# Issuing the two output stores of a pair from ScalarE instead of SyncE, in a two-layer graph attention kernel

## What is computed

```python
x = _layernorm(x + _L0_gnn_ref(x, adj, adj, Wq, Wk, Wv, bv, Wo, bo))   # scores + adj + adj, output projection
x = _layernorm(x + _L1_gnn_ref(x, adj, Wq, bq, Wk, bk, Wv, bv, beta))  # scores + beta*adj, masked where adj <= 0
# scores = q k^T * scale + bias;  probs = softmax(scores);  out = probs v
# layernorm(x) = (x - mean) / sqrt(var + 1e-5)
```

## Time and profile before

| | us |
|---|---|
| median of 3 runs | 2331.73 (2331.39 to 2332.79) |
| the profiled execution | 2332.92 |
| its span, first to last instruction | 2331.1 |
| PE busy | 2136.1 (92%) |
| DVE busy | 1876.7 (81%) |
| ACT busy | 1844.8 (79%) |
| POOL busy | 1558.9 (67%) |

### The profile page before, as it was taken

One profiled execution on the slowest core, in us unless ns is written; L12 is line 12 of the kernel. 1 busy time (PEld: TensorE's weight loads), 2 busy tenths in 40 slices (PEclk: granted clock), 3 DMA queues, 4 the chain that ended last, 5 costly groups with the idle time before them and its releaser, 6 DMA issues.

```text
span 2331.1 us, 86096 instructions
## 1 busy us (share of the span) xinstructions
PE 2136.1 (92%) x23808; PEld 1926.8 (83%) x23808; DVE 1876.7 (81%) x8451; ACT 1844.8 (79%) x7688; POOL 1558.9 (67%) x2188
## 2 busy tenths in 40 slices
PE   5899999999999999999999999999999999999973
PEld 5888888888888888888888888888888888888852
DVE  4688888888888888888888888888888888888763
ACT  5578888888888788788788788888888888887764
POOL 5666766776676776676676676676676676676652
PEclk9999999999999999999999999999999999999976
DMA  5255454454554554554554554544544544544443
GB/s 145 72 135 131 131 140 125 131 140 128 128 143 126 129 142 123 133 140 121 137 138 120 140 134 122 143 131 122 142 131 126 138 130 129 134 130 122 123 104 79
DMA packets 234654, 299.36 MB, mean 128 GB/s; under 512 B 26704, under 2 KB 226384, under 8 KB 234576
## 3 DMA queue, kind: packets, MB, share of 16 engines
q1 hardware_dynamic: 234576, 298.43, 49.4%
HBM read 46.67 MB, written 25.17 MB: 31 GB/s over the span
## 4 chain that ended last, share of the span: by engine, by line
PE 44%; issue 18%; ACT 15%; DVE 11%; POOL 8%; DMA 1%; ACTq 1%; DVEq 1%; POOLq 0%; SPq 0%
ACT prob L586 13%; PE r_bank L365 11%; PE r_bank L367 9%; PE r_bank L366 9%; PE s_bank L415 7%; DVE neg_s L697 5%; PE r_bank L431 4%; POOL flip L914 3%; PE r_bank L348 2%; DVE neg_max L697 2%; PE r_bank L358 1%; PE r_bank L443 1%; DVE y L763 1%; POOL rstd L863 1%; ACT o1T L558 1%
## 5 line engine op out<-in xcount | busy, mean ns | idle before, releaser
L586 ACT ACTIVATE prob<-neg_s,neg_max 128x128 f32<-128x128 f32 x3072 | 1192.1, 393 | 205.6 <-DVE neg_max L697 205.0
L697 DVE CUSTOM_DVE_ANT_0 neg_s<-s_bank,bias 128x128 f32<-128x128 f32 x3072 | 670.3, 286 | 145.8 <-PE s_bank L415 116.0
L586 ACT ACTIVATION_READ_ACCUMULATOR prob<-neg_s,neg_max 128x1 f32 x3072 | 589.9, 192 | 0.0
L932 POOL TENSOR_TENSOR prob<-prob,inv_sum 128x512 f32<-128x512 f32 x384 | 389.3, 1043 | 15.5 <-DVE inv_sum L785 11.7
L914 POOL TENSOR_TENSOR flip<-neg_s 128x768 f32<-128x768 f32 x128 | 234.7, 1834 | 194.4 <-DVE neg_max L697 138.2
L365 PE MATMUL r_bank<-x1T_hi,w_hi 128*128 128x256 f32 x1152 | 358.2, 311 | 2.9 <-ACT k0T L547 1.6
L365 PE MATMUL r_bank<-xT_hi,w_hi 128*128 128x256 f32 x1152 | 351.4, 305 | 9.3 <-DVE xT_lo L719 9.3
L367 PE MATMUL r_bank<-xT_hi,w_lo 128*128 128x256 f32 x1152 | 327.3, 284 | 0.0
L366 PE MATMUL r_bank<-xT_lo,w_hi 128*128 128x256 f32 x1152 | 326.4, 283 | 0.0
L366 PE MATMUL r_bank<-x1T_lo,w_hi 128*128 128x256 f32 x1152 | 325.9, 283 | 0.0
L367 PE MATMUL r_bank<-x1T_hi,w_lo 128*128 128x256 f32 x1152 | 325.1, 282 | 0.0
(11 more groups left out here) (75 smaller groups left out, 5316.4 us busy)
## 6 DMA issues: line engine op xcount, KB each, us to landing
prob0T<-flip SPq DMA_DIRECT2D x512, 192.0 KB, 3.5
prob1T<-stage SPq DMA_DIRECT2D x512, 192.0 KB, 3.7
x_in<-in_x_dram SPq DMA_DIRECT2D x128, 192.0 KB, 3.2
x_late<-x SPq DMA_DIRECT2D x64, 384.0 KB, 2.6
out_dram<-y SPq DMA_DIRECT2D x128, 192.0 KB, 2.3
adj<-in_adj_dram SPq DMA_DIRECT2D x256, 64.0 KB, 2.3
stage<-in_L_gnn_Wv_dram SPq DMA_DIRECT2D x2, 576.0 KB, 4.2
stage<-in_L_gnn_Wq_dram SPq DMA_DIRECT2D x2, 576.0 KB, 5.3
```

The costliest lines, as they stand in the source:

```text
L586: act.activation(prob[layer][:, h, :], neg_s[layer][:, h, :], ACT.Exp, bias=neg_max[layer][:, h:h + 1], scale=-1.0, accum_out=row_sum[laye ...
L697: dve.tensor_tensor_reduce(neg_s[layer][:, h, :], s_bank[b][:, (h // HC) * N:(h // HC + 1) * N], bias[layer][q.parity][:, g, :], -1.0, BIG ...
L932: pool.tensor_tensor(prob[0][:, hs, :], prob[0][:, hs, :], inv_sum0[:, hs].unsqueeze(2).to_broadcast([P, HC, N]), ALU.mult).then_inc(probn ...
```

## The change

Both `store` calls leave SP's `body`. A `store` of the same form is defined on ACT, and is called once behind `qk_out(1, prev2, 5)`, one activation behind `norm_apply1` of graph 1, and once behind `exps(1, prev2, 0, 0, 2)`, two exponentials behind `norm_apply1` of graph 0. It waits on `x2_done`, the semaphore that `norm_apply1` raises. On SP, `keep_x1` gets a `sem_inc` between its two waits.

```diff
-            def store(q, g):                      # on SP
-                if q.valid():
-                    sp.wait_ge(x2_done, q.count(1, g, 1))
-                    sp.dma_start(out[bass.ds(2 * q.index() + g, 1)].rearrange("g (j a) d -> a j (g d)", j=NB), y[1][:]
-                                 ).then_inc(stored, 16)
             def keep_x1(q):
                     sp.wait_ge(x1_done, q.count(1, 1, 1))
+                    sp.sem_inc(sp_passed, 1)
                     sp.wait_ge(y1_done, q.plus(-2).count(1, 1, 1))
             def body(r, off):                     # on SP
                 n = Pair(r, off)
-                store(n.plus(-4), 1)
                 keep_x1(n.plus(-2))
...
                 load_adj1(n.plus(-1))
-                store(n.plus(-3), 0)
                 spread_probs(0, n, 1)
...
+            def store(q, g):                      # on ACT
+                if q.valid():
+                    act.wait_ge(x2_done, q.count(1, g, 1))
+                    act.dma_start(out[bass.ds(2 * q.index() + g, 1)].rearrange("g (j a) d -> a j (g d)", j=NB), y[1][:]
+                                  ).then_inc(stored, 16)
...
                 norm_apply1(prev4, 1)
                 qk_out(1, prev2, 5, r)
+                store(prev4, 1)
                 exps(1, prev3, 1, 0, 5)
...
                 norm_apply1(prev3, 0)
                 exps(1, prev2, 0, 0, 2)
+                store(prev3, 0)
                 qk_out(0, nxt, 4, r)
```

More of the change, by code:

```diff
@@ L195, in build @@
         ident_done = sem("ident_done")
-        dve_passed, pool_passed = sem("dve_passed"), sem("pool_passed")
+        dve_passed, pool_passed, sp_passed = sem("dve_passed"), sem("pool_passed"), sem("sp_passed")
         xt_done, x1t_done = sem("xt_done"), sem("x1t_done")
```

## The result

The changed kernel is slower: a median of 2371.97 us (2369.99 to 2375.61, 4 runs) against 2332.26 us of the kernel before on the same chip, a ratio of 1.0171 with a 95% interval of 1.0154 to 1.0189, so 39.7 us lost. The forecast was 2389, 57 us lost; the time lies in the range of 2350 to 2430, and the loss is 0.70 of the forecast one.

What follows compares the result with a forecast made beforehand. The prediction took ACT, where the stores go, as the engine others wait for. Delays of 0.60 us (graph 1) and 0.34 us (graph 0), 0.94 us a pair over 61 pairs, gave 57 us: 2389 us, range 2350 to 2430.

Steps and rivals of the forecast that it cites:

- What bounds the kernel: ACT is the engine others wait for: DVE for its last exponential, then PE for y; PE for the o1T copy.
- SP's relief at nothing: Removing 128 waits and issues from SP gains nothing, since its spreads wait for DVE's flip 128 times of 128.
- Graph 1, 0.76 us late: First half of a turn: behind the store, ACT's exponential would begin at 1033.11 instead of 1032.35.
- The slack of graph 1: ACT's 0.16 us idle for PE before q0T, the only slack before the exponentials; leaves 0.60 us of delay.
- Graph 0, 0.34 us: Second half of a turn: the store delays ACT's k0T copy by 0.34 us, with no gap before o1T.
- The sum: Both delays add up to 0.94 us in a pair; 61 pairs counted, 57 us in all.
- The drain: Rival: ACT's DMA begins only when activations already handed over have ended; 2.07 us a pair, 2458 us; chance 0.14.
- Hidden on ScalarE: Rival: ACT's sequencer has activations in stock while it issues, so no change, 2332 us; chance 0.11.
- The faster case: Rival: SP comes free and POOL's fold gets the layer 0 spread earlier; 2306 us if ACT's issues are hidden; chance 0.05.

Runs made afterwards that it cites:

- no cover: Changed kernel with both stores on ACT directly behind their apply, nothing between: 2437.67 us against 2332.60 for the kernel before, ratio 1.0445.
- two issues: Changed kernel with each store issued as two halves of 192 columns, the same bytes: 2464.12 us against 2332.60 for the kernel before, ratio 1.0560.
- The far places: Changed kernel with stores five (graph 1) and six (graph 0) activations behind the apply: 2332.03 us against 2331.98 for the kernel before, ratio 1.0002.

## Why the prediction came out as it did

**What bounds the kernel: right.** DVE's wait for the exponentials and PE's wait for o1T were the two doors, and the stretches behind the two stores are the only ones that grew.

**SP's relief at nothing: right.** The flip still came last in 128 of 128 cases, and the kernel without stores gained nothing.

**Graph 1, 0.76 us late: right for the turn shown, a little high in the mean.** In the turn shown it was 0.75 us, made of 0.19 instead of 0.21 us to the issue, 0.58 instead of 0.63 us of issue and 0.24 instead of 0.18 us to the next activation: errors that cancel. Over the 47 turns it alternates between about 0.64 and 0.75 us from one turn to the next, 0.69 us in the mean. Why it alternates, and why this restart is longer than SP's, was not tested.

**The slack of graph 1: mis-sized.** I took 0.16 us from the bracket before q0T and so 0.60 us net; the net is 0.44. The bracket counts idle time from the end of the record before, a row-sum read that ended at 1034.38. But the next activation does not wait for that end: in the run without gaps the next instruction starts 0.10 us before it, as q0T itself does in the changed kernel (read from 1051.67 for 0.19, q0T at 1051.77). The room was 0.26 us here and 0.25 us in the mean, and that is what was absorbed: 0.69 us late at the first exponential, 0.44 us longer in the stretch. It holds for the longer delays too. With no cover the first exponential is 0.99 us late and the stretch 0.72 us longer, with two issues 1.41 and 1.16 us, so that 0.27 and 0.26 us were absorbed.

**Graph 0, 0.34 us: mis-sized.** It was 0.24 in the turn, mainly because the issue took 0.55 us where the same store on SP took 0.65.

**The sum.** 0.94 us in a turn was forecast and 0.65 measured. Of the 0.29 us between, 0.07 belong to the lateness of graph 1, 0.09 to its slack, 0.10 to graph 0, and some 0.03 to the other stretches, which got shorter by that much. Times 61 that is 18 us, the distance between the 57 us forecast and the 40 measured. That the two prices add up was right, by the kernels with one store each.

**The rivals.** The drain is excluded: the second exponential started at 1032.16, during the issue that ran from 1032.05 to 1032.60. Hidden on ScalarE was false for these places and true for others. The far places show that ScalarE can have such a stock: seven instructions are handed over and not yet started when the issue begins at 1032.14, and one is running. It is the program order, by the wait on the apply, that kept this stock from forming. The faster case fell with the kernel without stores.

## What to carry to other kernels

A DMA issue is not counted as busy, but here ScalarE's queue handed over nothing while it lasted: behind the apply of graph 1 the issue took 0.58 us, and the next activation began 0.24 us after its end. Before moving one onto a computing engine, take its start (the end of what it waits for), add the issue and the restart, about 1.0 us here, and subtract the time of the activations that stand between the awaited result and the issue in the program. If others wait for the work behind it, each turn pays the rest; here one activation more in between brought the loss from 40 us to about 1. And look first whether the engine that is relieved was ever late: a long wait at the old place (413.8 us) says nothing if the next wait simply takes it over. Read slack from the start of one instruction to the start of the next, and compare it with a run without gaps: by the ends of the records it was 0.16 us here, in truth 0.25.

## What the runs showed of the hardware

The same store was issued faster by ScalarE than by SyncE: in the kernel with graph 1 on ScalarE the median issue was 564 ns there and 652 ns on SP, and in the kernel with graph 0 on ScalarE 564 and 634 ns. An issue on ScalarE cost more than its own record of 0.55 us, 0.71 us of the queue when a second one followed, and the landing took 2.2 us against 2.3. ScalarE's stores went through a DMA queue of their own (q10 in the page, 25.17 MB; q1 has the others, 273.25 MB) and took nothing from SP's that shows: the spreads landed within 0.1 us of before (3.5 and 3.8 us in the median against 3.5 and 3.7). The copy keep_x1 did land later after its issue, 3.9 instead of 2.6 us. The place behind the spread is the likely reason: it is 3.9 us also in the kernel without stores, and 2.6 us in the kernel with only graph 0 on ScalarE, where it stands at its old place. Nobody waited for it.
